# A linear-attention stage whose value-spreading transfers write each head's own columns only, with no mask multiplication on GpSimd

## The reference

```
x = layernorm(x + attention_0(x))      # "lion" linear attention, 16 heads of 8 numbers
x = layernorm(x + experts_0(x))        # top 2 of 8 experts
x = layernorm(x + attention_1(x))      # gated delta rule
x = layernorm(x + experts_1(x))        # top 1 of 8 experts
```

```
A_f = einsum('bhik,bhjk->bhij', r * exp(cf), k * exp(-cf))     # used where i >= j
A_b = einsum('bhik,bhjk->bhij', r * exp(-cb), k * exp(cb))     # used where i < j
A   = where(lower, A_f, A_b)
y   = einsum('bhij,bhjk->bhik', A, v)
```

## Time and profile before

| | us |
|---|---|
| median of three runs | 1179.0 |
| lowest, highest | 1173.12, 1182.3 |
| profiled execution, span from the first to the last instruction | 1182.9 |
| busy in that span: PE, DVE, ACT, POOL | 926.2, 773.2, 556.9, 491.2 |
| mean granted clock of TensorE, share of full speed | 0.854 |

### The profile page before, as it was taken

How to read it: one execution, slowest core, us unless ns; L and a number is a source line. 1 busy time by engine, 2 the same in 40 slices (tenths; PEclk the granted TensorE clock), 3 DMA queues, 4 the chain that set the end, 5 groups by cost and what they waited for, 6 DMA issues and landing times. The chain is left out here.

```text
span 1182.9 us, 34132 instructions
## 1 busy us (share of the span) xinstructions
PE 926.2 (78%) x12733; PEld 656.9 (56%) x12734; DVE 773.2 (65%) x2236; ACT 556.9 (47%) x1120; POOL 491.2 (42%) x596
## 2 busy tenths in 40 slices
PE   5789887978794299999188897938899997416995
PEld 2356555555572198899134445737555563216885
DVE  3576889888945255555158886953588878733664
ACT  1346555655531055555157774233565455305664
POOL 0111255236526244454257762011034444643776
PEclk9799888988955599999689998965999987757998
DMA  2222133305501222222334323023222234011220
GB/s 87 46 64 64 33 69 83 74 27 138 178 23 42 55 62 59 57 55 55 92 80 91 87 40 136 3 86 94 67 63 57 65 93 143 14 33 45 54 56 20
DMA packets 122118, 79.50 MB, mean 67 GB/s; under 512 B 46980, under 2 KB 108522, under 8 KB 121601
## 3 DMA queue, kind: packets, MB, share of 16 engines
q1 hardware_dynamic: 115328, 64.95, 20.7%
q0 software_dynamic: 6656, 12.70, 3.4%
HBM read 49.05 MB, written 27.51 MB: 65 GB/s over the span
## 5 line engine op out<-in xcount | busy, mean ns | idle before, releaser
L1134 ACT ACTIVATE bx_h<-bx_up,bx_cur 128x128 f32<-128x128 f32 x288 | 82.1, 368 | 104.0 <-PE bx_up L1105 104.0
L573 POOL DMA_INDIRECT regions_b<-a_xo,a_seat x64 | 63.9, 998 | 145.2 <-DVE a_seat L877 128.1
L688 ACT ACTIVATE a_at<-a_scores 128x1024 f32<-128x1024 f32 x64 | 65.5, 1024 | 103.0 <-PE a_scores L447 102.5
L1063 POOL DMA_INDIRECT chosen_b<-bx_ys,bx_to x72 | 76.4, 1060 | 89.8 <-DVE bx_ys L1177 89.3
L442 PE MATMUL a_scores<-a_rk,a_kx 32*128 32x128 f32 (+3 forms) x1024 | 65.5, 323 | 41.2 <-DVE a_at L895 33.1
L442 PEld LDWEIGHTS a_scores<-a_rk,a_kx 32*128 32x128 f32 x1024 | 49.4, 215 | 65.0 <-DVE a_at L895 44.9
L1105 PE MATMUL bx_up<-bx_xT,bx_cur 128*128 128x128 f32 x576 | 82.4, 287 | 2.1 <-issue 0.4
L1087 PE MATMUL bx_down<-bk_w,bx_h 128*128 x576 | 82.1, 286 | 0.3 <-ACT bx_h L1134 0.3
L600 POOL TENSOR_TENSOR a_vx<-a_vx,a_con 128x2048 f32<-128x2048 f32 x8 | 36.1, 4513 | 104.7 <-DMA a_vx<-lion_values 104.6
L1105 PEld LDWEIGHTS bx_up<-bx_xT,bx_cur 128*128 128x128 f32 x576 | 71.0, 194 | 11.3 <-DVE bx_cur L1150 5.0
L1087 PEld LDWEIGHTS bx_down<-bk_w,bx_h 128*128 128x128 f32 x576 | 69.7, 191 | 3.5 <-issue 0.4
(11 more groups left out here) (431 smaller groups left out, 2533.1 us busy)
## 6 DMA issues: line engine op xcount, KB each, us to landing
a_vx<-lion_values SPq DMA_DIRECT2D x32, 256.0 KB, 4.5
bx_xs<-regions_b SPq DMA_DIRECT2D x72, 65.0 KB, 1.8
bk_w<-in_b_w SPq DMA_DIRECT2D x16, 256.0 KB, 5.7
c_part<-chosen_b SPq DMA_DIRECT2D x16, 256.0 KB, 4.0
space<-in_d_w SPq DMA_DIRECT2D x16, 256.0 KB, 6.0
dx_xs<-regions_d SPq DMA_DIRECT2D x40, 65.0 KB, 1.8
a_xp<-in_a_xT SPq DMA_DIRECT2D x8, 256.0 KB, 4.2
a_xr<-in_x SPq DMA_DIRECT2D x8, 256.0 KB
```

Of the source, the lines that this page charges most:

```text
L573: nc.gpsimd.indirect_dma_start(route["regions"], bass.IndirectOffsetOnAxis(ap=seat[b][:, k, t:t + 1], axis=0), xo[b][k][:, t, :], None).th ...
L688: op(at[m % 2][:], S4[:, :, 0:320].rearrange("p g (q k) -> p g q k", q=2)[:, :, :, 0:P], ACT.Copy).then_inc(s_ata, 1)
L1063: nc.gpsimd.indirect_dma_start(dest, bass.IndirectOffsetOnAxis(ap=to[u][:, 0:1], axis=0), ys[u][:], None, bounds_check=dest.shape[0] - 1, ...
L1134: i = op(h[u % 2][:, f, :], BU[u % 2][:, f * P:(f + 1) * P], act_fn, bias=cur[u % 2][:, FC * P + f:FC * P + f + 1])
```

## The change

The value columns are stored in another order: column j of head group g, once at 32g + j, now lies at 4j + g. The 32 columns of head h (eight from each of four head groups) are then next to each other, at 32h to 32h+31. This order is set once, where ACT writes the weight `wT[:, 2, :]`. The four transfers to `a_vx` now carry to partitions 32h to 32h+31 only columns 32h to 32h+31; the rest of both buffers is set to zero once, by two POOL instructions at the start, on which SP waits before the first store. The POOL multiplication, its mask and its semaphore are gone, and PE waits for the transfers themselves. PE picks a head group's columns with a step of 4 elements, in `attend` as the stationary operand, and in `states` as the moving operand.

```
-    c["vhead"] = (p // 32)[:, None] == ((p % 32) // 8)[None, :]
...
+        s_vz = sem("lion_v_zeros_set")
...
+        by_group = lambda a: a.rearrange("p (j g) -> p g j", g=4)
...
                 for h in range(4):
-                    sp.dma_start(vx[b][32 * h:32 * h + 32], v_chunks[b]).then_inc(s_vxp[b], 16)
+                    own = slice(32 * h, 32 * h + 32)
+                    sp.dma_start(vx[b][own, :, own], v_chunks[b][:, :, own]).then_inc(s_vxp[b], 16)
...
+            sp.wait_ge(s_vz, 2)
             spread_values(0)
...
-                    i = mm(X2[:, t * P:(t + 1) * P], kt[:, t ^ 1, :], vt[:, t ^ 1, :], start=True, stop=True)
+                    i = mm(X2[:, t * P:(t + 1) * P], kt[:, t ^ 1, :], by_group(vt[:, t ^ 1, :]), start=True, stop=True)
...
                 if m == 0:
                     pe.wait_ge(s_st, n + 1)
-                    pe.wait_ge(s_vx, n + 1)
+                    pe.wait_ge(s_vxp[b], 64 * (n // 2) + 64)
...
-                        i = mm(Y[32 * g:32 * g + 32, t * P + 32 * q:(t + 1) * P], vx[b][:, 4 * t + q, 32 * g:32 * g + 32],
+                        i = mm(Y[32 * g:32 * g + 32, t * P + 32 * q:(t + 1) * P], by_group(vx[b][:, 4 * t + q, :])[:, g, :],
                                at[m % 2][:, g, q % 2, 0:k], start=False, stop=False, skip_group_check=True)
...
-            def mask_values(n):
-
-                b = n % 2
-                pool.wait_ge(s_vxp[b], 64 * (n // 2) + 64)
-                nc.gpsimd.tensor_tensor(vx[b][:], vx[b][:], C["vhead"].unsqueeze(1).broadcast_to([P, GTOK // 32, P]),
-                                        ALU.mult).then_inc(s_vx, 1)
-
-            pool.wait_ge(s_w, NW)
-            mask_values(0)
+            for b in range(2):
+                nc.gpsimd.memset(vx[b][:], 0.0).then_inc(s_vz, 1)
             for n in range(NG):
                 if n >= 2:
                     scatter(n - 2)
-                if n + 1 < NG:
-                    mask_values(n + 1)
                 if n:
                     norm(n - 1)
...
-            op(wT[:, 2, :], Y[:, P:2 * P], ACT.Copy).then_inc(s_wv, 1)
+            op(by_group(wT[:, 2, :]), Y[:, P:2 * P].rearrange("p (g j) -> p g j", g=4), ACT.Copy).then_inc(s_wv, 1)
```

More of the change, by code:

```diff
@@ L250, in lion_stage @@
         s_v, s_vt = sem("lion_v_projected"), sem("lion_v_rows")
-        s_vd, s_vxp, s_vx = [[sem(f"lion_v_{n}_{i}") for i in range(2)] for n in ("stored", "spread")] + [sem("lion_v_chunks")]
+        s_vd, s_vxp = [[sem(f"lion_v_{n}_{i}") for i in range(2)] for n in ("stored", "spread")]
+        s_vz = sem("lion_v_zeros_set")
         s_kk, s_kd, s_ktp, s_kt = sem("lion_keys_scaled"), sem("lion_r_scaled"), sem("lion_keys_transposed"), sem("lion_key_rows")
@@ L466, in attend @@
                     for g in range(4):
-                        i = mm(Y[32 * g:32 * g + 32, t * P + 32 * q:(t + 1) * P], vx[b][:, 4 * t + q, 32 * g:32 * g + 32],
+                        i = mm(Y[32 * g:32 * g + 32, t * P + 32 * q:(t + 1) * P], by_group(vx[b][:, 4 * t + q, :])[:, g, :],
                                at[m % 2][:, g, q % 2, 0:k], start=False, stop=False, skip_group_check=True)
                     for g in range(4 if q else 0):
-                        i = mm(Y[32 * g:32 * g + 32, t * P:t * P + 32 * q], vx[b][:, 4 * t + q, 32 * g:32 * g + 32],
+                        i = mm(Y[32 * g:32 * g + 32, t * P:t * P + 32 * q], by_group(vx[b][:, 4 * t + q, :])[:, g, :],
                                at[m % 2][:, g, q % 2, k:P], start=False, stop=(q == 3), skip_group_check=True)
```

## The result

The changed kernel takes 1134.94 us (median of 4 runs, 1133.11 to 1135.5) against 1177.2 us for the kernel before, measured beside it. The ratio is 0.9635, with a 95% interval of 0.9604 to 0.9667: 3.7% faster. The profiled execution spans 1133.1 us. The forecast was 1132 us.

What follows compares the result with a forecast made beforehand. Bound: PE waiting once a group for DVE, whose spread POOL's mask stretches, which also halves PE's clock. 33.4 (waits) - 1.5 (norm) + 17.5 (clock) - 1.4 (states) - 1 (weights) = 47.0 us; 1179.0 - 47 = 1132 us, range 1120 to 1163 us.

Steps and rivals of the forecast that it cites:

- The waits: PE's waits for DVE at each group's first scores: without the mask stretching DVE's spread, 33.4 us gained.
- The norm in group 2: POOL's norm, now earlier, meets DVE's spread in group 2 and gives back 1.5 us; bounds 0 and 2.2.
- Rival A: Norm takes the mask's place in holding DVE's spread, by the locked port pair: 1163 us; chance 0.13.
- The clock: Without the wait PE keeps full clock through sub-step 0 of groups 1 and 3 to 7: 17.5 us gained.
- Rival B: Gaps remain at the turn of the group and PE's clock does not return: 1148 us; chance 0.15.
- `states` with its step: Moving operand of states read with a step of 4: eight matmuls cost 0.7 us more a group.
- Attend with its step: Stationary operand of attend, 1792 loads of 32 columns, read with a step of 4: 1 us lost.
- rival C: Attend's weight loads with a step no longer overlap, 65 us more on PE: 1197 us; chance 0.05.
- Transfers and fills: Smaller spreading transfers stay covered, and two fills of about 2.5 us each follow the set-up: cost 0.

Runs made afterwards that it cites:

- after_times_ones: Changed kernel with a GpSimd multiplication of a_vx by a tensor of ones put back at the old mask's place: 1162.26 us.
- after_scale_one: Changed kernel with a GpSimd multiplication by the constant 1.0, reading one tensor, put at the old mask's place: 1168.07 us.
- before_no_mask: Kernel before with the mask multiplication left out and nothing else changed, so values are not masked: 1127.78 us.
- after_attend_plain: Changed kernel with attend reading 32 neighbouring channels as weights, without the step (wrong channel selection): 1134.62 us.
- before_mask_late: Kernel before with its whole mask multiplication put behind norm in GpSimd's list: 1181.1 us.
- GpSimd's 16 pieces: Kernel before with the mask multiplication written as 16 instructions of 128 elements: 1168.92 us at the old place, 1179.22 us behind norm.
- after_states_plain: Changed kernel without the step in the moving operand of states; DVE puts the columns back while masking: 1133.38 us.

## Why the prediction was right, and where its terms were off

**The waits.** Forecast 33.4 us, from 35.0 us of stretch less 0.2 us for each of eight groups. The stretch fell by 34.35 us; by the same 0.2 us that is 32.8 us. What holds DVE was read correctly, and after_times_ones and after_scale_one bring it back in the groups where POOL's long instruction meets the spread.

**The norm in group 2.** Forecast 1.5 us given back. It was 0.14 us, although the norm did run across the spread. The rows on line 583 had already spoken for that; the four of line 593 last 0.8 us each and held DVE by no more than that 0.14 us in all. Rival A (1163 us) rested on them and fell with them.

**The clock.** Forecast 17.5 us net, which with the 0.7 us of `states` in six groups is 21.7 us without any step. The mechanism came as forecast; the size can be read in two ways. By the medians it was put too high: PE kept busy in the wait gained 14 us, and the kernel before without its mask gained 50.5 us, of which 32.2 us are the waits (44.07 - 10.30 us of stretch, less 1.6 us), so 18.3 us are the clock's, 3.4 us less than forecast. By the traces it was not: from group 0's spread to the next stage before_no_mask is 54.8 us shorter than the kernel before, 22.6 us beside the waits. The forecast was read from that long execution; where its 6 to 8 us lie no run shows.

The single groups do not depend on the total. In a middle group it is 40.9 - 33.2 - 4.8 = 2.9 us, where 2.9 + 0.7 = 3.6 us were forecast, and in group 6 it is only 1.4 us. Together groups 3 to 6 gave 4.6 us less than forecast. Groups 0 and 2, which were given nothing, gave 3.7 us: the wait that the forecast left standing in group 2 went, and its sub-step 0, at 0.50 from 121.1 to 127.9 us before, is at 1.00 after. So the total of the traces came out right partly by luck. Sub-step 0 shows where half of the 0.7 us is: the mixing was put at 1.6 us, half of its 3.05 us before, and takes 1.95 us at full clock, 178.80 to 180.75 us. The 3.05 us (166.54 to 169.59 us) were not all cold, since the stretch at 0.50 ends at 168.9 us; halving them was the slip. The last group, left open in the range, did not help: it is at 0.50 from 289.5 us on. Rival B fell with the clock of 1.00 at every turn from group 1 on.

**`states` with its step.** A smaller miss: 0.7 us forecast from the 1.7 and 1.0 ns a column of the earlier trace rows, 0.91 us measured. Against its own plain reading (1.16 us) the moving operand with a step of 4 floats costs 227 against 112 ns a matmul, from the start times within the eight: the double, not 1.7 times. (The 121 ns of the prediction and of the expectation are the weight loads', 0.97 us for eight.)

**Attend with its step.** Forecast 1 us, and the trace has it as 0.06 us per half tile with 24 matmuls and 0.11 us with 32, 5.4 us over all 64. Of that the period shows 0.31 us a group, 2.5 us in all, and the median nothing (after_attend_plain, 1134.6 us). So rival C's mechanism, loads that no longer overlap, did not come, and the rule on cachelines in the Trainium skill (Advanced Engine Details and Errata, section "Memory Cachelines") shows at the moving operand (2.07 instead of 1.16 us for eight matmuls) and only just at the stationary one (0.06 and 0.11 us per half tile), and at full clock alone: in group 0, at half clock, `states` takes 2.17 instead of 2.08 us.

**Transfers and fills.** Cost 0 forecast. The two fills take 3.56 us together instead of 5, under the set-up. The spreading lands earlier, not later: in groups 0 to 2 of after_times_ones, where POOL's start shows it, 3.8 to 4.1 us after its issue, against some 7 us in the kernel before. Since nothing waits for it, that is worth nothing.

**The sum.** Forecast 47.0 us; measured 42.3 us between the medians, 4.7 us less. Without steps and collision the forecast was 33.4 + 21.7 = 55.1 us, and the kernel without the mask gave 50.5 us: by this account the waits and the clock were 4.6 us too high. The steps were put at 0.7 x 8 + 1 = 6.6 us; they are 5.4 us by the period (0.67 x 8) and 7.2 us by the medians (1134.94 - 1127.78 us, from different batches), and the collision of 1.5 us did not come; the last 1.0 us is the difference of the two batches (1178.25 and 1177.2 us for the kernel before). The traces give another account. The two profiled executions differ by 49.8 us; 2.25 us of that are the start (below) and -1.4 us the later stages, so the stage from group 0's spread on gained 49.0 us, 2.0 us more than forecast, which is the collision and a little of the steps. The two accounts differ because the terms were read from an execution some 6 us longer than the median. The time came out nearer than the gain, 1134.94 against 1132 us, because the forecast started from a median of 1179.0 us and the kernel before gave 1177.2 us beside the changed one. That part is luck.

## What to carry to other kernels

A long GpSimd instruction was dear here where VectorE's next one was a copy, a multiplication by a scalar or a `tensor_tensor` on SBUF alone, and free where VectorE read PSUM: read from the order of time on both engines what it meets, before moving or splitting it. Splitting a long one gives no sure turn to the other engine, and moving it back only works if its consumer is further off than its own length. In a middle group of this kernel a wait of 4.8 us on TensorE's path cost a further 2.9 us through the clock. A changed layout was paid at the moving operand, hardly at the weights.

## What the hardware showed that was not expected

- VectorE's instructions that a long GpSimd instruction held: the spread (one SBUF input), `tensor_tensor` on two SBUF inputs (3.21 instead of 0.68 us), a copy of 4 elements (4.02 us). Not held beside one of over 2.5 us, in any of the fourteen traces: instructions with an input in PSUM, which took at most 0.03 us more than elsewhere; and in after_times_ones the statistics of group 2, 0.28 us each at 101.4 to 102.0 us under a multiplication from 100.12 to 103.95 us.
- GpSimd's 16 pieces start 0.41 us apart when they are alone or keep VectorE out, and up to 0.88 us apart beside instructions on 512 elements. Whether VectorE got its turn varied from group to group in one execution; what decides it stays open.
- The same instruction on GpSimd took 3.82 us with ones as second input, in the changed kernel, and 4.52 us with the head mask, in the kernel before. Why was not tried.
- The start of the program comes in two lengths. Group 0's spread begins at 37.7 to 38.9 us in some profiled executions and at 40.7 to 40.8 us in others, in kernels that are the same up to there (before 40.73 us, before_mask_late 38.79 us). Most of the difference arises between 16.5 and 20 us, where TensorE is warm in the one and cold in the other; eight small matmuls take 0.96 us in the changed kernel and 1.72 us in after_states_plain:

```profile
16.86 0.96 PE L425 MATMUL a_scores<-a_gw,a_xp 128*128 128x8 f32 x8
```

```profile
17.32 1.72 PE L425 MATMUL a_scores<-a_gw,a_xp 128*128 128x8 f32 x8
```

- They stand 112 and 213 ns apart, so one execution has TensorE at 2.4 GHz there, for 3.4 us by its clock record (16.4 to 19.9 us), and the other has not. The view gives the granted clock as 1.00 in both, and also in the 4 us before, where two matmuls of 512 columns take 2.07 us (1.04 us at full clock, above). The clock records begin only at 16.4 us in the one trace and at 35.5 us in the other, and where there is none the view counts 1.00. At the start of a trace the duration of a matmul is to be believed, not the row of the clock.
